# Weights of the later stages fetched in quarters, and the feed-forward stage's x turned by the DMA transpose

## The reference

```python
x = _ln(x + _mha(x, x, sa_wq, ..., mask), ln1_g, ln1_b)           # "SA"
x = _ln(x + _mha(x, memory, ca_wq, ..., None), ln2_g, ln2_b)      # "CA"
h = jax.nn.relu(_linear(x, ff_w1, ff_b1))                         # 512 -> 2048, "UP"
x = _ln(x + _linear(h, ff_w2, ff_b2), ln3_g, ln3_b)               # 2048 -> 512, "DOWN"
```

## Time and profile before

| | |
|---|---|
| median of 3 runs | 3950.6 us (3949.4 to 3952.84) |
| profiled execution, its own time | 3951.78 us |
| span from its first to its last instruction | 3950.0 us |
| PE busy | 3764.8 us, 95% of the span |
| DVE, ACT, POOL busy | 2734.5, 2235.5, 1853.9 us |
| mean granted TensorE clock | 0.991 of full speed |
| transfers | 586.72 MB, mean 149 GB/s |

### The profile page before, as it was taken

One profiled execution on the slowest core, in us unless ns is written; L12 is line 12 of the kernel. 1 busy time (PEld: TensorE's weight loads), 2 busy tenths in 40 slices (PEclk: granted clock), 3 DMA queues, 4 the chain that ended last, 5 costly groups with the idle time before them and its releaser, 6 DMA issues.

```text
span 3950.0 us, 63494 instructions
## 1 busy us (share of the span) xinstructions
PE 3764.8 (95%) x20700; PEld 2795.9 (71%) x20700; DVE 2734.5 (69%) x5801; ACT 2235.5 (57%) x4852; POOL 1853.9 (47%) x1905
## 2 busy tenths in 40 slices
PE   9999999999999998999999998999999979999999
PEld 6767776767777766766677766666666658888887
DVE  6666666677777778888888877888888843333334
ACT  6555555555555556888887777777777741111111
POOL 5444344344344345777777665676766621011001
PEclk9999999999999999999999999999999989999999
DMA  6676676555545466776666446777666671111000
GB/s 200 195 201 194 193 207 180 141 146 138 135 130 134 125 196 168 176 181 173 174 174 170 125 146 177 193 193 190 179 167 171 162 225 59 36 48 44 33 33 32
DMA packets 842517, 586.72 MB, mean 149 GB/s; under 512 B 611792, under 2 KB 660944, under 8 KB 841168
## 3 DMA queue, kind: packets, MB, share of 16 engines
q1 hardware_dynamic: 824400, 532.33, 50.6%
q10 hardware_dynamic: 17792, 50.33, 3.7%
HBM read 197.68 MB, written 238.55 MB: 110 GB/s over the span
## 4 chain that ended last, share of the span: by engine, by line
PE 37%; ACT 6%; DVE 6%; issue 5%; POOL 5%; DMA 3%; SPq 1%; DVEq 0%; POOLq 0%; ACTq 0%
PE psV L1526 5%; POOL QS L2343 4%; PE psT L1495 4%; PE psS L1474 3%; PE psS L1420 3%; PE psS L1421 3%; PE psS L1419 3%; PE psJ L1419 2%; PE psJ L1421 2%; PE psJ L1420 2%; ACT PR L1802 2%; PE psT L1419 2%; PE psT L1421 2%; PE psT L1420 2%; DVE PR L1998 1%
## 5 line engine op out<-in xcount | busy, mean ns | idle before, releaser
L2343 POOL TENSOR_SCALAR QS<-QK 32x1024 fp32r<-32x1024 f32 (+2 forms) x1152 | 1231.9, 1069 | 865.6 <-DVE QK L2012 405.7
L1802 ACT ACTIVATE PR<-PR,MN 128x512 f32<-128x512 f32 x1536 | 1101.5, 718 | 606.8 <-DVE MN L1994 458.4
L1994 DVE CUSTOM_DVE_ANT_0 PR<-psS,RAW 128x512 f32<-128x512 f32 x1024 | 693.9, 682 | 395.0 <-PE psS L1471 302.9
L1495 PE MATMUL psT<-ID,PR 128*128 128x128 f32 x3912 | 598.1, 276 | 76.8 <-ACT PR L1802 73.7
L1495 PEld LDWEIGHTS psT<-ID,PR 128*128 128x128 f32 x3912 | 473.1, 141 | 211.1 <-ACT PR L1802 122.2
L1526 PE MATMUL psV<-plain 128*32 128x512 f32 (+1 forms) x3072 | 509.6, 611 | 30.1 <-DMA plain<-split_rows 22.6
L1474 PE MATMUL psS<-QS 128*128 128x512 f32 x1024 | 456.5, 447 | 28.2 <-DVE PR L1998 14.4
L1998 DVE TENSOR_SCALAR_CACHE_REDUCE PR<-psS 128x512 f32<-128x512 f32 x512 | 344.9, 683 | 120.5 <-PE psS L1474 117.9
L1841 ACT ACTIVATE PR<-psS,COLS 128x512 f32<-128x512 f32 x128 | 88.3, 690 | 547.0 <-PE psS L1421 542.2
L2090 DVE COPY plain<-psT 128x512 f32<-128x512 f32 x530 | 361.5, 682 | 0.0
L2064 DVE CAST QK<-PR 128x512 fp32r<-128x512 f32 x128 | 59.9, 468 | 398.5 <-ACT PR L1841 353.8
(11 more groups left out here) (142 smaller groups left out, 8411.6 us busy)
## 6 DMA issues: line engine op xcount, KB each, us to landing
split_rows<-plain SPq DMA_DIRECT2D x366, 256.0 KB, 2.7
split_rows<-RAW SPq DMA_DIRECT2D x192, 256.0 KB, 2.6
x<-Y SPq DMA_DIRECT2D x96, 256.0 KB, 2.4
RAW<-x SPq DMA_DIRECT2D x96, 256.0 KB, 3.8
W<-kept ACTq DMA_DIRECT2D x12, 2048.0 KB, 11.7
Y<-x SPq DMA_DIRECT2D x96, 256.0 KB, 3.6
kept_c<-R SPq DMA_DIRECT2D x32, 512.0 KB, 4.1
kept<-ROWS SPq DMA_DIRECT2D x32, 512.0 KB, 3.8
```

Of the source, the lines that this page charges most:

```text
L1495: mm = nc.tensor.transpose(dst[:, kt * P:(kt + 1) * P], prob(st, k)[:, kt * P:(kt + 1) * P], ID[:, :])
L1802: nc.scalar.activation(prob(st, k), prob(st, k), ACT.Exp, bias=MN[:, k % 8:k % 8 + 1], scale=-1.0, accum_out=row_sums(st, SM, g)[:, qt, j: ...
L1994: nc.vector.tensor_tensor_reduce(out=prob(st, k), in0=psS[:, n % 2], in1=FB[:, k % NT], scale=-st.scale, scalar=BIG, op0=ALU.add, op1=ALU. ...
L2343: nc.gpsimd.tensor_scalar(to, pair, 1.0, 1.0, ALU.mult, ALU.mult).then_inc(stacked, 1)
```

## The change

**Takes in parts.** A matrix whose entry in `TAKES` has a tuple of four slots is fetched as four transfers of 512 KB, one for each slice kt, each at its own slot. CA's V, FF's U0, U1, U2 and D0 also move to other slots; U2 moves from the last CA batch into FF's first.

**x of FF turned by transfers.** For batches 1 to 7 of FF, SP loads x into `FB` (`f_load`), POOL splits its words into two 16-bit planes in `OG` (`split_rows_of_x`), SP writes these to `x_rows` (`f_bounce`) and reads them back through the DMA transpose into `RAW` (`f_fetch`), ScalarE makes the high half and VectorE the low half (`f_hi_part`, `f_lo_part`). The turned x alternates between `OT` and `xT` (`ff_x`), so that both halves are made during the batch before, beside `relu(8)` to `relu(11)` and `hidden(10)` to `hidden(13)`. The transposes on TensorE are gone. In the loops SP issues the new x transfers ahead of the result's stores.

```diff
 TAKES = {
     ("last", 1): [("SA", "Q", 15), ("SA", "K", 19.2), ("SA", "V", 20.7)],
-    ("first", 2): [("SA", "O", 26)],
-    ("last", 2): [("CA", "Q", 42.2), ("CA", "K", 44.7), ("CA", "V", 45.2)],
-    ("first", 3): [("CA", "O", 26)],
-    ("last", 3): [("FF", "U0", 40.7), ("FF", "U1", 42.2), ("FF", "U2", 44.7), ("FF", "D0", 44.9)],
-    "ff": [("FF", "D1", 71.2), ("FF", "U3", 71.3), ("FF", "D2", 71.4), ("FF", "D3", 90)],
+    ("first", 2): [("SA", "O", (26, 29, 32, 35))],
+    ("last", 2): [("CA", "Q", 42.2), ("CA", "K", 44.7), ("CA", "V", (24, 27, 30, 33))],
+    ("first", 3): [("CA", "O", (26, 29, 32, 35))],
+    ("last", 3): [("FF", "U0", (24, 27, 30, 33)), ("FF", "U1", (44, 46, 48, 50)), ("FF", "D0", (52, 54, 56, 58))],
+    "ff": [("FF", "U2", (64, 65, 66, 67)), ("FF", "D1", 71.2), ("FF", "U3", 71.3), ("FF", "D2", 71.4), ("FF", "D3", 90)],
 }
...
-        add(61 + tt if tt < 2 else 94 + 2 * tt, "LOAD_X", tt, 1)
-        add(97 + 2 * tt, "X_TURN", tt, 1)
-        add(97 + 2 * tt, "X_HI", tt, 1)
-        add(98 + 2 * tt, "X_LO", tt, 1)
+        for step, slot in zip(("F_LOAD", "F_PLANES", "F_BOUNCE", "F_FETCH", "F_HI", "F_LO"), (80, 82, 84, 88, 96, 98)):
+            add(slot + 2 * tt, step, tt, 1)
...
+            def f_load(b, tt):
...
+                    sp.wait_ge(f_planes, before(b - 1, tt) + 1)
+                sp.dma_start(FB[:, tt], dram["x3"][b, tt * P:(tt + 1) * P, :]).then_inc(f_full[tt], 16)
+            def f_bounce(b, tt):
+                sp.wait_ge(f_planes, before(b, tt) + 1)
...
+                sp.dma_start(x_rows[tt], planes()).then_inc(f_bounced[tt], 16)
+            def f_fetch(b, tt):
+                sp.wait_ge(f_bounced[tt], 16 * b)
...
+                    sp.wait_ge(f_lo, before(b - 1, tt) + 1)
+                sp.dma_start_transpose(raw_turned(tt).bitcast(U16), x_rows[tt].rearrange("q h k -> (q h) k")).then_inc(
+                    f_fetched[tt], 16)
...
             for r in range(B - 2):
+                ff_inputs(r + 2)
                 ff_stores(r)
                 ff_residuals(r + 1)
-                ff_inputs(r + 2)
...
-                if f == 0:
+                if f == 0 and first:
                     pe.wait_ge(j_evac, tal["j"].done(tal["j"].marked(("x", NT - 1))))
+                elif f == 0:
+                    pe.wait_ge(f_lo, before(b, NT - 1) + 1)
...
-                for f in range(2):
-                    x_turn(2 * f)
-                    x_turn(2 * f + 1)
-                    down(NF - 2 + f)
+                for f in range(NF - 2, NF):
+                    down(f)
...
+                if kt is None:
+                    act.dma_start(f32(both).rearrange("p h k c -> p (h k) c"),
+                                  kept[n // KT].rearrange("h k p c -> p (h k) c")).then_inc(w_taken[place], 16)
+                else:
+                    act.dma_start(f32(both[:, :, kt]), kept[n // KT, :, kt].rearrange("h p c -> p h c")).then_inc(
+                        w_taken[place], 16)
...
+            def split_rows_of_x(b, tt):
...
+                    pool.wait_ge(f_bounced[(tt - 1) % NT], 16 * (b if tt else b - 1))
...
+                nc.gpsimd.tensor_scalar(planes(), FB[:, tt].bitcast(U16).rearrange("p (k h) -> p h k", h=2), 1.0, 1.0,
+                                        ALU.mult, ALU.mult).then_inc(f_planes, 1)
```

More of the change, by code:

```diff
@@ L151 @@
     ("last", 1): [("SA", "Q", 15), ("SA", "K", 19.2), ("SA", "V", 20.7)],
[L152 to L156 removed]
[5 rows of a table added]
 }
 def take_steps(key):
[L161 removed]
+    return [(slot, "W_TAKE", (stage, kind, kt if isinstance(slots, tuple) else None), None, 0, None)
+            for stage, kind, slots in TAKES.get(key, []) for kt, slot in enumerate(slots if isinstance(slots, tuple) else (slots,))]
+IN_PARTS = {(stage, kind) for takes in TAKES.values() for stage, kind, slots in takes if isinstance(slots, tuple)}
 def weight_steps(key):
@@ L960, in build @@
         qs_zero = sem("qs_zero")
+        f_full = [sem(f"f_full{i}") for i in range(NT)]
+        f_planes = sem("f_planes")
+        f_bounced = [sem(f"f_bounced{i}") for i in range(NT)]
+        f_fetched = [sem(f"f_fetched{i}") for i in range(NT)]
+        f_hi = sem("f_hi")
+        f_lo = sem("f_lo")
         def w_place(place, part):
@@ L1015, in qk, with ff_x, planes, raw_turned @@
             return FB.bitcast(F32R) if bank(st, g) else QK
+        def ff_x(b):
+            return OT if b % 2 else xT
+        def planes():
+            return OG[:, :].bitcast(U16).rearrange("p (h k) -> p h k", h=2)
+        def raw_turned(tt):
+            return RAW[:, tt].rearrange("p (k t) -> p k t", k=KT)
+        def before(b, tt):
+            return NT * (b - 1) + tt
         def row_sums(st, t, g):
@@ L1160, in take_count @@
             kinds = [tile[:2] for tile in KEPT[::KT]]
-            return 16 * sum(1 for other in kinds[:kinds.index((stage, kind)) + 1] if PLACE[other] == PLACE[stage, kind])
+            return sum(16 * KT if other in IN_PARTS else 16 for other in kinds[:kinds.index((stage, kind)) + 1]
+                       if PLACE[other] == PLACE[stage, kind])
         block = stack.enter_context(nc.Block())
@@ L1380, in ff_inputs @@
                 for tt in range(NT):
-                    load_x("x3", b, tt)
+                    f_load(b, tt)
+                for tt in range(NT):
+                    f_bounce(b, tt)
+                for tt in range(NT):
+                    f_fetch(b, tt)
             def ff_residuals(b):
@@ L2118, in pair_tile, with f_lo_part @@
                                         ALU.mult).then_inc(side_ready, 1)
+            def f_lo_part(b, tt):
+                dve.wait_ge(f_hi, before(b, tt) + 1)
+                hi, lo = (ff_x(b)[:, p, :, tt * P:(tt + 1) * P] for p in range(2))
+                nc.vector.tensor_tensor(lo, raw_turned(tt), f32(hi), ALU.subtract).then_inc(f_lo, 1)
             def run(steps, batch):
                 for step, k, st, off, at in steps:
-                    if step == "P_LO":
+                    if step == "F_LO":
+                        f_lo_part(at, k)
+                    elif step == "P_LO":
                         prob_lo(st, k, batch + off if at is None else at)
@@ L2193, in _, with batch @@
             dve.wait_ge(rows_full, rows_seen[0] + 48)
-            def batch(nxt):
+            def batch(b):
                 for f in range(NF):
@@ L2203, in batch @@
                         normalise(f - 6)
-                if nxt:
-                    for tt in range(NT):
-                        x_lo_part(tt, xT)
+                    if 10 <= f < 10 + NT and b < B - 1:
+                        f_lo_part(b + 1, f - 10)
+                if b < B - 1:
                     totals()
-            for _ in range(B - 2):
-                batch(True)
-            batch(False)
+            for b in range(1, B):
+                batch(b)
             for tt in range(NT):
@@ L2409, in _ @@
             passes(run, settled)
-            for _ in range(B - 2):
+            for r in range(B - 2):
+                for tt in range(NT):
+                    split_rows_of_x(r + 2, tt)
                 for tt in range(NT):
```

83 lines of the change are left out of this document (55 added, 28 removed).

## The result

The changed kernel takes 3917.11 us (median of 5 runs, 3913.12 to 3920.56), the one before 3950.6 (5 runs, 3949.4 to 3952.84): ratio 0.9917, 95% interval 0.9905 to 0.9928. The forecast was 3914.

The account below looks back on a forecast made before the run. The prediction took TensorE, busy 95%, to bound the kernel, with three stalls set by transfers and FF by TensorE's own instructions. 12.2 + 26.8 - 2 = 37.0 us off gave 3914 us on the median, range 3902 to 3934.

Parts of the forecast that it names:

- FF, -12.2 us: FF: removing TensorE's transposes of x in seven batches, 1.74 us each, takes 12.2 us off the path.
- The cover in FF's first batch: FF's first batch: the turned x is ready before `up(0)` of batch 1; cost 0, cover 18 us.
- The stalls, -26.8 us: SA's O, CA's O and CA's last batch: takes in parts and spread give back 26.8 us of 34.6.
- The ceiling of CA's last batch: End of CA's last batch: at most 20.8 us to gain, from TensorE's idle time and work at lower clock.
- U0 goes to slots 24 to 35, where only the ordinary traffic is: CA's last batch: U0's new slots were said to hold no traffic beyond the ordinary.
- the 16 taken: CA's last batch: 16 us of the 20.8 come back, some lag staying beside U1 and D0.
- The 10.8 us for the O's: SA's and CA's O: parts spread over 12 slots give back 10.8 of 13.8 us.
- The rule against the change: All takes: 1 MiB or more per DMA; by it only the transposes gain, less 2 us, stalls kept or spread.
- The parts, +2: ScalarE's queue: 28 issues for 7 and a possibly later `relu` cost 2 us, between 0 and 8.
- The signs named ahead: FF period 87.1 us; bounces 3 to 5 us; window 3160 to 3200 over 35 us busy, clock near 1.00; issues 0.4 us.
- half relieved: The stalls: parts still meet bounces, so half of the 26.8 us is left, 3927 us; chance 0.25.
- spread, not relieved: The stalls: the same engine time is taken from bounces, so every stall only moves, 3940 us; chance 0.07.

Follow-up runs that it names:

- e1: The kernel before with only the takes in parts and at their new slots, FF's x still turned on TensorE: 3925.9 us.
- e11: The kernel before with 13 of its 16 takes cut to an eighth of their bytes, same slots and waits: 3920.7 us.
- e5: The changed kernel with the four x loads in CA's last batch moved from slots 28 to 28.3 to slots 34, 36, 38 and 49.4: 3910.4 us.
- e3: The changed kernel with each cut matrix fetched whole, 2 MB at the slot of its first part: 3919.6 us.
- e4: The changed kernel with matrices cut in four, but all four parts at the old slot of the whole matrix: 3940.0 us.
- e8: The changed kernel with both O's in parts and CA's V, U0, U1, D0 and U2 whole at their first part's slot: 3915.5 us.
- e9: The changed kernel with x loads at slots 34, 36, 38, 49.4 of CA's last batch and CA's V, U0, U1, D0, U2 whole: 3911.0 us.
- e7: The changed kernel with SA's O and CA's O fetched whole, 2 MB at slot 26: 3931.2 us.
- e10: The changed kernel with x loads at slots 34, 36, 38, 49.4 of CA's last batch and both O's whole at slot 26: 3920.4 us.
- e12: The changed kernel with 13 of its 16 takes at an eighth of their bytes, issues and slots kept: 3906.3 us.

## Why the prediction was right, and where it was not

**FF, -12.2 us: right**, 12.8 measured in the segment. The period is 87.04 us where 87.1 was forecast; (88.86 - 87.04) x 7 = 12.7. TensorE's 40.00 of 40, no transpose of x after 3175.3 us (L1514 in the changed kernel) and the split (1.05 us in the median for 1.07) stand as forecast. For the split a nearer row stood in the trace of the kernel before than the one that was used, the same 128x1024 uint16 split on other engines (ScalarE 1.05 us, L1811; VectorE 0.69, L2098). The cover in FF's first batch was given as 18 us. By the prediction's own terms it is less: 28 us, less six waits of 3, less a fetch of 3.4, leave 6.6. The trace agrees with that: the last fetch is issued at 3271.30, the four low halves run from 3286.33 to 3289.66, `up(0)` of the next batch starts at 3294.7 (VectorE's timeline; all that reads `OT` on TensorE):

```profile
3286.33 3.33 DVE L2199 TENSOR_TENSOR OT<-RAW,OT 128x512 fp32r<-128x512 f32 x4
```

```profile
L1481 PE MATMUL psS<-OT,W x48: 389/389/389, 3294.7 to 3351.1; 128*128 128x512 f32 x48
```

They end 5 us ahead. The fetch took 4.2 us and had landed long before, so the 5 us are the cover of the two halves, not of the transfers.

**The stalls, -26.8 us: the right places, too large a size, and the reason right only in part.** The three segments of the profiled executions give 3.2 + 7.3 + 11.8 = 22.2; from the medians it is 33.5 - 12.8 = 20.7, and 20.2 for the parts alone (e1). Three terms of it:
- The ceiling of CA's last batch was 20.8, worked out against an ordinary stretch's 1.52 us of idle time. The end of the batch has less to do for TensorE in any case; e11 puts it at 17.0 (with x loaded at slot 28, as before; e5, which moves those loads too, gains 17.4). The ceilings of the O's, 6.7 and 7.1, measured 6.1 and 7.7.
- "U0 goes to slots 24 to 35, where only the ordinary traffic is" is the sentence that failed. SP issues 1 MB of x at slot 28. The meeting costs 4.2 to 5.5 us (148.2 to 144.0 and 142.7), which is what CA last, with 11.8, is short of the 16 taken, within the measured ceiling of 17.
- The 10.8 us for the O's agree with the one profile (10.4), and not with the means over all kernels, 4.9. In CA O executions with the same takes differ by up to 5.8 us (42.6 and 48.4), so the agreement with the profile is partly luck; the whole times (6 to 13 us) leave the size open.

**Why it works** was put down to the size of the parts ("a bounce then loses at most a part's 1.7 us"). In CA's last batch most of it comes from the new places of the matrices, with or without the cut (e3, e4). By the prediction's reason whole matrices at the new slots (e3) should have given away most of the gain, and 3935 us was named for them; they took 3919.6. So the forecast would have come out about as well without the cut that it was argued from, and that is luck. Only at CA's O do the chains show the cut itself at work. **The rule against the change** (the Trainium skill, DMA: Bandwidth & Descriptors, Rules for kernel authors, 1 MiB or more per DMA) gave the transposes alone less 2 us. With every matrix but the two O's whole, e8 and e9 are as fast as the changed kernel and e5 within their intervals, so the rule costs nothing to follow there; at the O's, e7 and e10 were slower with 2 MB at once. Breaking it cost nothing that e12 against e11 shows, since nobody waited for a matrix.

**The parts, +2: nearer 0.** Each issue took under 0.5 us apart from FF's `x3` (5.54 us for 5.23), and e12 against e11 leaves no cost. CA's V, whose move was counted as nothing, shows nothing: between "SA" and "CA O" lie 114.8 us before and 114.4 now.

**The signs named ahead.** Bounces near 3 to 5 us at the O's: 4.83 and 5.02 on the chain. In CA's last batch the median bounce landed in 4.0 us, but the longest took 7.5 (11.9 before), just over the 7 that was to prove the spreading wrong, and the fetch behind the x loads took 10.99. TensorE over 35 us in 3160 to 3200 and a clock near 1.00: no, 32.50 and 0.91; e5 has 35.06 and still 0.91.

**The sum.** By medians, and with the parts taken as free, FF gave 0.6 us more than forecast, the parts cost 2 less, and the stalls gave 6.1 less (20.7 for 26.8): 37.0 + 0.6 + 2 - 6.1 = 33.5. So two small terms that erred the other way hid part of the miss in the large one. The profiled execution saved more, 38.7 us, of which 5.2 are a CA mid that was shorter by no doing of the change. Of the rivals, "half relieved" would have left 13.4 us of the stalls and "spread, not relieved" none.

## What to carry to other kernels

Here large background transfers hurt small ones that the chain waits for by standing next to each other, more than by being large: piled takes made the batch 159 us, whole ones apart 147, parts 144. So first move them apart, then cut those that still meet a waiting transfer, and list what every queue issues in the new place, since the move's own collision (with 1 MB of x on SP) took back 4 to 5 of 17 us. Measure a ceiling taken from idle time against the same stretch with the bytes taken away (17.0 us), not against an ordinary stretch (20.8). Where TensorE had no idle time at all, in FF, the instructions taken from it came off the time one for one (12.8 us for 12.2).

## What was not expected

Middle batches of CA, with one and the same program, take 108.1 to 108.5, 109.9 to 110.6 or 111.4 to 112.7 us from one context take to the next, over all these profiles (the last interval, 105.9 to 106.5 in each, is left out). The chain of the changed kernel over its middle batches shows what the longer ones wait for:

```profile
2509.74 9.39 DMA RAW<-in_w
...
2728.02 10.51 DMA RAW<-in_w
2839.61 9.54 DMA RAW<-in_w
```

This is the load of a raw weight that is still to be split and kept, and ScalarE's 2 MB of context is issued within 0.6 us of it:

```profile
2620.03 0.33 ACTq L1769 DMA_DIRECT2D R<-kept_c  x1
2728.29 0.33 ACTq L1769 DMA_DIRECT2D R<-kept_c  x1
2840.15 0.33 ACTq L1769 DMA_DIRECT2D R<-kept_c  x1
```

The batches that begin at 2509.69, 2728.29 and 2840.15 took 110.3, 111.9 and 110.1 us, the one at 2620.03, without such a load on the chain, 108.3. The other profiles bear it out: seven kernels have four such loads on the chain and a CA mid of 655.7 to 660.0 us (before, e3, e4, e7, e9, e10, e12), six have three and 653.7 to 656.9, and e1 has two and the shortest, 651.5. The load itself is what differs. At 2620.03 it was issued 0.26 us ahead of the take, nearly as at 2728.29 (0.27), and landed in 3.5 us for 10.5; why, these rows don't show. Again a small load that the chain waits for meets 2 MB, and it costs 2 to 4 us a batch by these rows; moving the context's take away from the load was not tried. The prediction took the middle of CA for ordinary and never looked at its chain.
